# The last pair of blocks of the down product as rounded parts and rests, for experts 1 to 5, and list products in another order

## The chip, the cores and the metric

The kernel runs on one core of a Trainium2 chip. The metric is the device time of one execution in microseconds (us), as the median of three runs.

## What is computed

A cross-attention layer with heads mixed before and after the softmax, and then a layer of eight experts with a balanced assignment, on two batches of 1024 rows of 256. Cut to what matters:

```
# attention: 16 heads of 64, context of 64 rows
attn = einsum(q, k); attn = einsum(attn, Wth1); attn = softmax(attn); attn = einsum(attn, Wth2)
x = x + einsum(einsum(attn, v), Wo)

# experts: E = 8, T = 2048 rows, each expert takes the 256 best of those not yet taken
y = layernorm(x); norm = layer_norm(y, ln_g, ln_b); scores = norm @ centroids.T
for e in range(E):
    s = where(taken, -inf, scores[:, e]); idx = top_k(s, 256); taken[idx] = True
h = layer_norm(y[idx of e], ln_g, ln_b)
h = gelu(h @ w1[e] + b1[e]) @ w2[e] + b2[e]          # 256 -> 1024 -> 256
x[idx of e] = x + y + h
```

## The kernel before

The program has a block per engine; each engine runs its own list of instructions in order and waits for semaphores of the others. There is no planner: the order is written out by hand in loops.

**Preparation and attention.** Fills (`for f in range(LATE)` on PE, ScalarE and VectorE) make the products of the key and value weights with the context, the head mixing, and their splits. `centre(h)` takes the mean out of the query weights: VectorE sums four blocks (L787), scales the sums (L789) and adds them to two blocks (L792), ScalarE to the other two (L608). Copies out of PSUM are by turns ScalarE's (even f) and VectorE's (odd f). Behind its copy f = 5 VectorE makes `mix` and two casts. Then come 16 tiles of 128 rows, in a pipeline of steps. In the last tiles VectorE counts the leading bytes of expert 0's scores: `count_bytes(t)` adds a comparison of 256 thresholds to `hist` for one tile; `first_totals()` on PE sums `hist` over the partitions, and `first_two()` on VectorE finds the first two digits of the threshold from the sum.

**The expert stage.** A loop `for k in range(SLOTS)`, written out, runs on PE, VectorE, ScalarE and GpSimd (POOL); I call one pass a round. In round k, expert k's threshold is searched (8 steps r, each `compare` on VectorE, `total` on PE, `narrow` on VectorE; `select` and `ranks` at the end), expert u = k - 1 gets its list and its rows, and expert e = k - 2 gets its up and down products. Round 7 has no search; its list follows from what is left.

The list of an expert: VectorE's `lists` makes `Hoh` and `Loh` (L1114); POOL's `token_rows` makes `Htk` of them (L505); PE's `tokens` multiplies both (waits for Htk), VectorE's `lists_out` masks (L1121), PE's `spread` spreads, VectorE's `indices` makes `idx` (L1126, L1130); POOL's `gather` starts two gathering DMAs (L516). The rows are transposed on PE (L1491, two halves, in steps 4 and 5), scaled by ScalarE into `yT` and `yF` (L713), and POOL subtracts for the rests (`y_rest`, L532).

A product in f32 "by parts": an operand is split into a rounded part (type fp32r) and a rest, and `mm3` (all PE products have line L1233) multiplies rounded by rounded, rounded by rest and rest by rounded. The up products of all experts are by parts: ScalarE's `w1_high` rounds w1 (L700), POOL's `w1_rest` subtracts in four instructions of 128x512 (L526). The down products of experts 0 to 5 are whole f32 products of `hT` and `w2s`, 16 per expert (two halves `a` of the rows, eight blocks `f`), laid over steps 2 to 8 by `DOWN`. Those of experts 6 and 7 (`parted`) are by parts, from `hp` and `w2p`: ScalarE writes gelu into a PSUM bank, and VectorE's `hidden_split` makes both parts from there (L1148, L1150), as `w2_rest` does for w2 (L1138).

POOL's order in a round k with u between 1 and 6: `token_rows(u)`, `w1_rest` 0, `gather(u)`, `w1_rest` 1 to 3, `y_rest(u)`, `bias(u)` (L540), `scatter(k - 3)` (two DMA issues, L547). ScalarE's: `hidden` of the later blocks (Gelu, L742), `w1_high(k)`, `rows(u)`, `hidden` of the first blocks of u. Memory of the experts: `hT` has two buffers by parity, `w2s` too; w2 of expert e is loaded (L408) when expert e - 2's down products are done.

## Time and profile before

| | |
|---|---|
| median of 3 runs | 309.21 us (308.43 to 309.61) |
| profiled execution | 308.5 us, of which the span from the first to the last instruction is 306.7 |
| granted TensorE clock, mean | 0.992 of full speed |
| busy: PE, PE's weight loads | 287.6 us (94%), 249.2 us (81%) |
| busy: VectorE, ScalarE, POOL | 233.1 (76%), 148.7 (48%), 197.5 us (64%) |
| chain that ended last | PE 77%, VectorE 8%, POOL 5%, DMA 4% |

Preparation lasts to about 51 us, attention to 162, the expert stage to the end. Busy time is that in which an instruction of the engine is under way; matmuls overlap, so twelve with 280 ns each take far less than twelve times that, and the pace is the distance of their starts. "Idle before" and the name behind an arrow say how long the engine stood before an instruction and who let it go on.

### The profile page before, as it was taken

To read this page: it belongs to the slowest core of one execution; us is meant where nothing else is said; L and a number is where in the kernel's file an instruction comes from. 1 tells how busy PE (TensorE), PEld (TensorE's weight loads), DVE (VectorE), ACT (ScalarE), POOL (GpSimd) and SP (SyncE) were. 2 spreads that over 40 slices of the span, in tenths; PEclk is the share of its full clock that TensorE was granted. 3 is DMA by queue.
4 is the path that set the end of the run, shared out by engine and by line. 5 is a ranking of instruction groups with operands and counts; after the bars stand their busy time and mean duration, and the time that the engine had idled before them with its cause. 6 is when DMAs were issued, how large, how long until landed. Compare 5 with 4: busy or idle time off the path is not lost.

```text
span 306.7 us, 6418 instructions
## 1 busy us (share of the span) xinstructions
PE 287.6 (94%) x2034; PEld 249.2 (81%) x2034; DVE 233.1 (76%) x808; ACT 148.7 (48%) x267; POOL 197.5 (64%) x247
## 2 busy tenths in 40 slices
PE   6999999999999999999988779999999999999990
PEld 2989998999999999999983228797979797989990
DVE  0579879999988888888877878687878787548650
ACT  1257646355445555555546523535353545474720
POOL 8200213468987888876742785758788878787951
PEclk9999999999999999999999999999999999999996
DMA  6996000991001000000016330474737474622020
GB/s 254 357 366 229 1 2 17 366 335 39 35 34 37 34 34 34 34 34 34 34 71 205 115 94 1 97 250 104 275 102 276 118 260 134 246 68 71 34 79 26
DMA packets 21770, 37.85 MB, mean 123 GB/s; under 512 B 2417, under 2 KB 14961, under 8 KB 21361
## 3 DMA queue, kind: packets, MB, share of 16 engines
q1 hardware_dynamic: 19184, 31.22, 29.4%
q0 software_dynamic: 2560, 6.31, 6.8%
q8 instruction: 14, 0.23, 0.3%
q14 instruction: 12, 0.09, 0.1%
HBM read 31.23 MB, written 6.29 MB: 122 GB/s over the span
## 4 chain that ended last, share of the span: by engine, by line
PE 77%; DVE 8%; POOL 5%; DMA 4%; issue 3%; ACT 1%; SPq 0%; POOLq 0%; DVEq 0%
PE pair L1233 67%; PE pair L1309 4%; PE pair L1283 2%; DMA wk_s<-wk_dram 2%; DVE cmpb L1019 1%; POOL w2p L556 1%; PE pair L1491 1%; DMA G<-rows_scratch,idx 1%; PE pair L1321 1%; POOL G L516 1%; DMA out_dram<-G,idx 1%; DVE wneg L787 1%; POOL out_dram L547 1%; POOL yT L532 1%; PE pair L1449 1%
## 5 line engine op out<-in xcount | busy, mean ns | idle before, releaser
L1233 PE MATMUL pair<-yT,w1p 128*128 128x256 f32 x384 | 53.2, 289 | 0.2
L1233 PE MATMUL pair<-Bm,pT 128*128 128x256 f32 (+1 forms) x384 | 49.9, 285 | 0.2 <-ACT pT L634 0.2
L1233 PEld LDWEIGHTS pair<-yT,w1p 128*128 128x128 f32 x384 | 48.3, 189 | 1.0 <-POOL yT L532 0.3
L1233 PE MATMUL pair<-Am,xTp 128*128 128x512 f32 (+1 forms) x192 | 48.9, 402 | 0.0
L1233 PE MATMUL pair<-w2s,hT 128*128 128x256 f32 x192 | 47.2, 389 | 0.0
L1233 PEld LDWEIGHTS pair<-Bm,pT 128*128 128x128 f32 x384 | 46.6, 188 | 0.4 <-issue 0.4
L288 POOL TENSOR_TENSOR pr<-pr,rs 128x1024 f32<-128x1024 f32 (+1 forms) x16 | 31.2, 1951 | 21.9 <-DVE rs L877 15.3
L526 POOL TENSOR_TENSOR w1p<-w1s,w1p 128x512 fp32r<-128x512 f32 x32 | 40.0, 1276 | 5.7 <-ACT w1p L700 5.6
L1233 PEld LDWEIGHTS pair<-Am,xTp 128*128 128x128 f32 x192 | 35.0, 189 | 7.0
L742 ACT ACTIVATE hT<-pair,b1s 128x256 f32<-128x256 f32 x48 | 20.1, 470 | 34.6 <-PE pair L1233 34.6
L1233 PEld LDWEIGHTS pair<-w2s,hT 128*128 128x128 f32 x192 | 33.5, 191 | 4.2
L469 POOL TENSOR_TENSOR xTp<-xTs,xTp 128x256 fp32r<-128x256 f32 x16 | 11.9, 741 | 33.8 <-ACT xTp L601 33.8
L629 ACT ACTIVATE pr<-pr,r 128x1024 f32<-128x1024 f32 x16 | 18.4, 1152 | 27.9 <-DVE pr L922 27.9
L516 POOL DMA_INDIRECT G<-rows_scratch,idx x16 | 15.8, 984 | 15.2 <-DVE idx L1130 12.8
L1019 DVE TENSOR_SCALAR_CACHE_REDUCE cmpb<-pair 128x256 bf16<-128x256 f32 x48 | 23.5, 489 | 1.7
L918 DVE TENSOR_REDUCE mx<-pair 128x16 f32<-128x1024 f32 x16 | 19.5, 1218 | 4.2 <-PE pair L1233 4.0
L883 DVE TENSOR_TENSOR pT<-pair,pT 128x512 fp32r<-128x512 f32 x32 | 21.3, 669 | 0.3 <-ACT pT L634 0.3
L922 DVE TENSOR_TENSOR pr<-pair,mx 128x1024 f32<-128x1024 f32 x16 | 19.6, 1225 | 2.0 <-DVE mx L918 1.3
L870 DVE TENSOR_REDUCE sm<-pr 128x16 f32<-128x1024 f32 x16 | 19.3, 1206 | 1.3 <-ACT pr L629 1.1
L547 POOL DMA_INDIRECT out_dram<-G,idx x16 | 15.8, 989 | 6.8 <-issue 3.1
L713 ACT ACTIVATE yT<-pair,gbs 128x256 fp32r<-128x256 f32 x16 | 8.2, 559 | 23.8 <-PE pair L1491 23.8
L1233 PE MATMUL pair<-ones_b 128*128 128x512 bf16 x61 | 17.9, 413 | 1.5 <-DVE ones_b L776 1.5
(157 smaller groups left out, 571.3 us busy)
## 6 DMA issues: line engine op xcount, KB each, us to landing
w1s<-w_dram SPq DMA_DIRECT2D x8, 1024.0 KB, 5.0
w2s<-w_dram SPq DMA_DIRECT2D x7, 1024.0 KB, 6.2
rows_scratch<-row SPq DMA_DIRECT2D x16, 256.0 KB, 2.0
xs<-x_dram SPq DMA_DIRECT2D x1, 2048.0 KB, 16.7
xTs<-xT_dram SPq DMA_DIRECT2D x1, 2048.0 KB, 18.4
wk_s<-wk_dram SPq DMA_DIRECT2D x1, 1024.0 KB, 6.0
wv_s<-wv_dram SPq DMA_DIRECT2D x1, 1024.0 KB, 8.3
wqT_s<-wqT_dram SPq DMA_DIRECT2D x2, 512.0 KB, 9.7
```

What stands on the lines that cost most here:

```text
L288: return eng.tensor_tensor(p4, p4, rs[:, v, :].unsqueeze(1).unsqueeze(3).to_broadcast([P, end - first, H, K8]), ALU.mult)
L516: pool.indirect_dma_start(out=G[:, b, a, :], out_offset=None, in_=rows_dram, in_offset=bass.IndirectOffsetOnAxis(ap=idx[:, e, a:a + 1], ax ...
L526: nc.gpsimd.tensor_tensor(w1p[:, 1, v, c, half], w1s[:, v, c, half], w1p[:, 0, v, c, half].bitcast(f32), ALU.subtract).then_inc(e_w1l, 1)
L547: pool.indirect_dma_start(out=out, out_offset=bass.IndirectOffsetOnAxis(ap=idx[:, e, a:a + 1], axis=0), in_=G[:, b, a, C:], in_offset=None ...
L629: nc.scalar.activation(pr[:, v, :], pr[:, v, :], ACT.Exp, scale=r1[:, ds(t, 1)]).then_inc(s_exp, 1)
L742: nc.scalar.activation(to, bank[1 + g % 2][:, h * CAP:(h + 1) * CAP], ACT.Gelu_apprx_tanh, bias=b1s[:, e * FC + f:e * FC + f + 1]).then_in ...
L870: nc.vector.tensor_reduce(sm[:, v, :], pr[:, v, :].rearrange("p (g i k) -> p i g k", g=KG, i=H), AX.XY, ALU.add).then_inc(s_sum, 1)
L883: nc.vector.tensor_tensor(pT[:, 1, v, q], probs_bank(t, g)[:], pT[:, 0, v, q].bitcast(f32), ALU.subtract).then_inc(s_pTs, 1)
L918: nc.vector.tensor_reduce(mx[:, v, :], pair[v][:].rearrange("p (g i k) -> p i g k", i=H, k=K8), AX.XY, ALU.max).then_inc(s_mx, 1)
L922: nc.vector.tensor_tensor(pr[:, v, :].rearrange("p (g i k) -> p g i k", i=H, k=K8), pair[v][:].rearrange("p (g i k) -> p g i k", i=H, k=K8 ...
L1019: nc.vector.tensor_scalar(cmpb[:], search_bank(k)[:, 0:T2 * P], thr.bitcast(f32), 0.0, ALU.is_ge, ALU.add, accum_out=cntb[:]).then_inc(r_c ...
L1233: return nc.tensor.matmul(out_, l, r, start=start, stop=stop)
```

## The change

- **Down products.** For experts 1 to 5 (`quarter`), the blocks f = 6 and 7 of the down product are by parts, 2 x 2 products of three instructions each in place of whole f32 ones. `LAST_DOWN`, which puts block 0 of the second half ahead of blocks 6 and 7 of the first, holds for them too.
- **Their parts.** ScalarE applies bias and gelu to the two blocks twice: first into `hp` (rounded, places 4 to 7 by parity), then into `hT` as before. VectorE subtracts (`pair_rest`, in step 4 of round e + 2, behind `compare` and `turn`). ScalarE rounds the pair of w2 behind `w1_high` (with a wait for the load of w2), POOL subtracts (`w2_pair_rest`, behind `w1_rest` 3 and ahead of `y_rest`, in round e + 1). PE waits for both in `down`.
- **Waits for shared places.** `hidden_split` of expert 6's third and fourth pair and `w2_part(7, 2)` wait for the end of expert 5's down products.
- **Lists.** In round 2, `spread` follows the up product of block 6 and not of block 5. In round 7, `tokens` comes behind the last two down products and the first two up products of expert 6 (part 8) and not ahead of them, and `spread` behind part 9 and not ahead of it.
- **Preparation.** Of the first four blocks of query weights, ScalarE centres three and VectorE one (two and two before). `mix` and the two casts come behind copy f = 11.
- **First digits.** The last tile's comparison goes into `atleast` alone; PE sums `hist` of the other 15 tiles, and then `atleast` on top.

```diff
@@ gpsimd
+            def w2_pair_rest(e, v):
+                q = quarter_place(e)
+                pool.wait_ge(e_qh, e)
+                nc.gpsimd.tensor_tensor(w2p[:, 1, 1, q], w2s[:, v, FC - 2:FC], w2p[:, 1, 0, q].bitcast(f32),
+                                        ALU.subtract).then_inc(e_ql, 1)
...
+                        if quarter(e):
+                            w2_pair_rest(e, v)
@@ scalar
-                for j in (4 * h + 2, 4 * h + 3):
+                for j in (1, 2, 3) if h == 0 else (6, 7):
...
+                if quarter(e) and g == FC // 2 - 1:
+                    for h in range(2):
+                        f = 2 * g + h
+                        nc.scalar.activation(hp[:, 0, 4 + v * 2 + h, :], bank[1 + g % 2][:, h * CAP:(h + 1) * CAP],
+                                             ACT.Gelu_apprx_tanh,
+                                             bias=b1s[:, e * FC + f:e * FC + f + 1]).then_inc(e_hq, 1)
...
+                if quarter(u):
+                    act.wait_ge(e_w2[u % 2], 16 * (u // 2 + 1))
+                    nc.scalar.activation(w2p[:, 1, 0, quarter_place(u)], w2s[:, u % 2, FC - 2:FC], ACT.Copy).then_inc(e_qh, 1)
...
+                        act.wait_ge(e_o, ST * PARTED)
                         w2_part(u, 2)
@@ vector
-                for j in (4 * h, 4 * h + 1):
+                for j in (0,) if h == 0 else (4, 5):
...
-                if f == 5:
+                if f == 11:
...
-            count_bytes(x)
+            dve.wait_ge(s_sc, T)
+            dve.wait_ge(r_hist, T - 1)
+            nc.vector.tensor_scalar(atleast[:], dig[:, 0, :], S[:, 0, x:x + 1], 1.0, ALU.is_le, ALU.mult).then_inc(r_last, 1)
...
-                if e > PARTED:
+                if e > PARTED or g >= 2:
                     dve.wait_ge(e_o, ST * e)
...
+            def pair_rest(e):
+                q = quarter_place(e)
+                dve.wait_ge(e_hs, FC * (e + 1))
+                dve.wait_ge(e_hq, 2 * e)
+                nc.vector.tensor_tensor(hp[:, 1, q, :], hT[:, e % 2, FC - 2:FC, :], hp[:, 0, q, :].bitcast(f32),
+                                        ALU.subtract).then_inc(e_hl, 1)
...
+                    if r == 4 and quarter(k - 2):
+                        pair_rest(k - 2)
@@ tensor
-                            pe.wait_ge(s_wcA, m // 2 + 2)
-                            pe.wait_ge(s_wcD, m // 2 + 2)
+                            pe.wait_ge(s_wcA, 3 if m == 0 else 5)
+                            pe.wait_ge(s_wcD, 1 if m == 0 else 3)
...
-                pe.wait_ge(r_hist, T)
-                mm(bank[5][:, 0:FIRST], ones_b[:, 0:P], hist[:], True, True).then_inc(r_first, 1)
+                pe.wait_ge(r_hist, T - 1)
+                mm(bank[5][:, 0:FIRST], ones_b[:, 0:P], hist[:], True, False)
+                pe.wait_ge(r_last, 1)
+                mm(bank[5][:, 0:FIRST], ones_b[:, 0:P], atleast[:], False, True).then_inc(r_first, 1)
...
-                if e == E - 1:
+                if e == E - 1 or quarter(e):
                     n = LAST_DOWN[n]
...
-                if parted(e):
+                if quarter(e) and f >= FC - 2:
+                    q = 4 + v * 2 + f - (FC - 2)
+                    pe.wait_ge(e_ql, e)
+                    pe.wait_ge(e_hl, e)
+                    last = mm3(bank[4 + a][:, 0:C], lambda i: hp[:, i, q, a * P:(a + 1) * P], lambda i: w2p[:, 1, i, q, :],
+                               False, f == FC - 1)
+                elif parted(e):
...
-                        if e == 0:
-                            list_of_tokens(k, gap, 1 - f % 2)
+                        if e == 0 and f == 5:
+                            list_of_tokens(k, gap, 0)
                         up(e, f)
                         if e > 0:
                             list_of_tokens(k, gap, f % 2)
+                        elif f == 6:
+                            list_of_tokens(k, gap, 1)
...
-                if k == E - 1:
-                    tokens(k)
                 expert_part(k, 8)
...
                 if k == E - 1:
-                    spread(k)
+                    tokens(k)
                 if searches(k):
                     ranks(k)
                 expert_part(k, 9)
+                if k == E - 1:
+                    spread(k)
```

The renaming of the loop variable `quarter` to `n` in `w1_rest` changes nothing.

## Rows read from the trace of the kernel before

**Rows 1.** The chain that ended last: start, us, what; the last turn from POOL to PE
```profile
268.16 3.56 DMA G<-rows_scratch,idx
271.77 0.44 PE pair L1491 x2
```
**Rows 2.** Busy time by stretch: us, engines with instructions, clock, DMA share, GB/s; round 5
```profile
233.82:248.92 15.10, 15.06 (x100) 12.95 (x100) 11.60 (x71) 7.10 (x14) 12.34 (x13) 1.00 0.59 189
```
**Rows 3.** Timeline of POOL, round 5: start, us, instruction, count, idle before and releaser
```profile
233.82 0.64 POOL L505 TENSOR_TENSOR Htk<-Hoh,cst 128x256 fp32r<-128x256 f32 x1
...
236.72 1.00 POOL L516 DMA_INDIRECT G<-rows_scratch,idx  x1 [1.02 <-DVE idx L1130]
...
239.00 3.72 POOL L526 TENSOR_TENSOR w1p<-w1s,w1p 128x512 fp32r<-128x512 f32 x3
243.65 1.41 POOL L532 TENSOR_TENSOR yT<-yF,yT 128x256 fp32r<-128x256 f32 x2 [0.93 <-ACT yF L713]
```
**Rows 4.** Timeline of PE, round 5: the product tokens, and the down products of step 5
```profile
234.51 0.44 PE L1233 MATMUL pair<-Htk,Loh 128*128 128x128 f32 x2
...
240.71 1.03 PE L1233 MATMUL pair<-w2s,hT 128*128 128x256 f32 x4
```
**Rows 5.** Timeline of PE: whole f32 down products in a row, and down products by parts
```profile
272.04 2.32 PE L1233 MATMUL pair<-w2s,hT 128*128 128x256 f32 x10
...
292.94 6.10 PE L1233 MATMUL pair<-w2p,hp 128*128 128x256 f32 x48
```
**Rows 6.** One line's instructions (ns least/median/most, when); timeline of POOL beside such subtractions
```profile
L1166 DVE TENSOR_TENSOR yT<-yF,yT x2: 412/938/1465, 285.4 to 286.7; 128x256 fp32r<-128x256 f32 x2
...
285.24 1.29 POOL L526 TENSOR_TENSOR w1p<-w1s,w1p 128x512 fp32r<-128x512 f32 x1
...
184.36 0.92 POOL L540 TENSOR_TENSOR G<-G,b2s 128x256 f32<-128x256 f32 x1
```
**Rows 7.** Single lines' instructions: ScalarE's Gelu and its copy of 128x512
```profile
L742 ACT ACTIVATE hT<-pair,b1s x48: 464/472/476, 186.3 to 267.8; 128x256 f32<-128x256 f32 x48
...
L727 ACT ACTIVATE w2p<-w2s x4: 633/638/641, 274.1 to 286.7; 128x512 fp32r<-128x512 f32 x4
```
**Rows 8.** Round 5: VectorE's turn in step 4; ScalarE's rows; a DMA issue's us to landing
```profile
240.06 0.16 DVE L1029 TENSOR_TENSOR pair<-pair,ics 128x1 int32<-128x1 int32 x1
...
242.10 1.02 ACT L713 ACTIVATE yT<-pair,gbs 128x256 fp32r<-128x256 f32 x2 [2.09 <-PE pair L1491]
...
w2s<-w_dram SPq DMA_DIRECT2D x7, 1024.0 KB, 6.2
```
**Rows 9.** Timeline of rounds 7 and 8, several engines
```profile
269.14 3.73 POOL L526 TENSOR_TENSOR w1p<-w1s,w1p 128x512 fp32r<-128x512 f32 x3
...
270.62 1.03 PE L1233 MATMUL pair<-w2s,hT 128*128 128x256 f32 x4
...
270.70 0.41 DVE L1114 TENSOR_TENSOR Loh<-cst,pair 128x256 fp32r<-128x256 f32 x1
...
276.77 4.49 PE L1233 MATMUL pair<-yT,w1p 128*128 128x256 f32 x36
...
282.87 0.69 DVE L1150 TENSOR_TENSOR hp<-pair,hp 128x512 fp32r<-128x512 f32 x1
...
283.61 3.80 PE L1233 MATMUL pair<-w2p,hp 128*128 128x256 f32 x30
```
**Rows 10.** Timeline of the preparation: VectorE's centring, PE's query and output weights
```profile
13.31 0.61 DVE L792 TENSOR_SCALAR wqT_s<-wqT_s,wneg 128x256 f32<-128x256 f32 x2
...
16.25 2.95 PE L1233 MATMUL pair<-kvT,wqT_s 64*128 64x128 f32 x48 [0.37 <-ACT wqT_s L608]
...
19.51 3.84 PE L1233 MATMUL pair<-kvT,wo_s 64*128 64x128 f32 x64 [0.31 <-DVE AB L813]
```
**Rows 11.** Timeline of PE at the end of the attention: the six filling products
```profile
161.21 1.46 PE L1233 MATMUL pair<-ones_b 128*128 128x512 bf16 x6
```
**Rows 12.** Timeline of PE, round 2: the product spread(1)
```profile
189.82 0.33 PE L1233 MATMUL pair<-Rt,exp_r 128*128 128x128 f32 x1 [0.47 <-DVE Rt L1121]
```

More of the change, by code:

```diff
@@ L193, in build @@
         r_R, r_Rt, r_Rx, r_Rxm = sem("r_R"), sem("r_Rt"), sem("r_Rx"), sem("r_Rxm")
-        r_idx = sem("r_idx")
+        r_idx, r_last = sem("r_idx"), sem("r_last_bytes")
         r_hist, r_hist0, r_first, r_firstj, r_firsts, r_atl = (sem("r_" + n) for n in ("hist", "hist_cleared", "first_totals", "first_sum", "first_state", "at_least"))
@@ L199, in build @@
         e_g = [sem(f"gathered{i}") for i in range(GB * ST)]
+        e_qh, e_ql, e_hq, e_hl = sem("w2_pair_high"), sem("w2_pair_rest"), sem("hidden_pair_high"), sem("hidden_pair_rest")
         e_yD = sem("first_rows_rest_dve")
@@ L246, in parted, with quarter, quarter_place @@
             return e >= PARTED
+        def quarter(e):
+            return 1 <= e < PARTED
+        def quarter_place(e):
+            return slice(4 + e % 2 * 2, 6 + e % 2 * 2)
         def part(e, kind, n):
@@ L519, in gather, with w1_rest @@
                     ).then_inc(e_g[ST * b + a], 16)
-            def w1_rest(e, v, quarter):
-                if quarter == 0:
+            def w1_rest(e, v, n):
+                if n == 0:
                     pool.wait_ge(e_w1h, e + 1)
-                c, half = quarter // 2, slice(quarter % 2 * F // 2, (quarter % 2 + 1) * F // 2)
+                c, half = n // 2, slice(n % 2 * F // 2, (n % 2 + 1) * F // 2)
                 nc.gpsimd.tensor_tensor(w1p[:, 1, v, c, half], w1s[:, v, c, half], w1p[:, 0, v, c, half].bitcast(f32),
                                         ALU.subtract).then_inc(e_w1l, 1)
+            def w2_pair_rest(e, v):
[3 more added lines that the diff above has]
+                                        ALU.subtract).then_inc(e_ql, 1)
             def y_rest(e, v):
@@ L561, in _ @@
                 if k == 0:
-                    for quarter in range(W1_PARTS):
-                        w1_rest(0, 0, quarter)
+                    for n in range(W1_PARTS):
+                        w1_rest(0, 0, n)
                     early_w2_rest(0)
@@ L575, in _ @@
                         if e > 0:
-                            for quarter in range(1, W1_PARTS):
-                                w1_rest(e, v, quarter)
+                            for n in range(1, W1_PARTS):
+                                w1_rest(e, v, n)
+                        if quarter(e):
+                            w2_pair_rest(e, v)
                     if e == E - 2:
@@ L585, in _ @@
                     if e == E - 2:
-                        for quarter in range(W1_PARTS):
-                            w1_rest(E - 1, (E - 1) % 2, quarter)
+                        for n in range(W1_PARTS):
+                            w1_rest(E - 1, (E - 1) % 2, n)
                 if 0 <= k - 3 < E:
```

## The prediction, made before the changed kernel was run

> **What bounds the kernel now.** I read the chain that ended last first, then the busy time by stretch, then the timeline of each engine in one round of the expert stage. A round is the piece in which one expert is searched for, the one before it gets its token list and rows, and the one before that its products. TensorE (PE) is busy nearly all of a round, 15.06 of 15.10 us, against 11.6 for VectorE (DVE), 7.1 for ScalarE (ACT) and 12.3 for GpSimd (POOL) [rows 2]. Read as shares, that says that PE is the bound and POOL has 2.8 us to spare. The chain says otherwise: its last stretch runs through POOL (the rest of the rows, the scatter issue, Htk, the gather), then through the gather's landing, and only at 271.77 back to PE, which stays on it to the end [rows 1]. So I follow POOL's queue. From Htk at 233.82 to the next at 248.92 it has two waits of size: 1.02 us before the gather, and 0.93 us before the rests of the rows [rows 3]. Everything behind the second follows without idle time, and the next Htk is ready just when PE wants it: PE's list product stands at 234.51, 0.05 after the end of its round's Htk (233.82 + 0.64) [rows 3, 4]. What POOL loses beyond 0.93 us in a round, PE therefore waits for.
>
> The wait before the gather can't absorb anything: it lies behind Htk, on the path Htk, PE's list product, DVE, PE's spreading product, DVE's indices, gather, and this path, 2.90 us from Htk to gather (236.72 - 233.82), moves along with Htk. POOL's own ring is thus 15.10 - 0.93 = 14.17 us, not 12.3.
>
> **Gain: the products.** A whole f32 product takes two instructions. Ten in a row take 2.32 us, less the last one's 0.38, over nine steps: 0.216 each, 0.432 for a product. Three products of parts: 48 instructions in 6.10, less 0.28, over 47: 0.124 each, 0.372 [rows 5]. For 4 products in each of 5 experts: 20 x 0.060 = 1.20 us of PE time less. This is worth something only where PE is the last to arrive. The Trainium skill (FP8 and Floating Point Precision, TensorE Precision Notes) counts a true f32 product as four passes; three instead of four would make it 0.324 and save 2.2 us in all. The rows have 0.372, and I go by them.
>
> **Cost: POOL.** w2_pair_rest adds one subtraction of 128x512 per round, put behind the last three of w1_rest. Those three take 3.72 us, a step of 1.24 [rows 3]. The wait of 0.93 behind them takes the most of it; 0.31 us are over.
>
> **Cost: the port between DVE and POOL.** pair_rest is a DVE subtraction with both inputs in SBUF (hT and hp). hidden_split keeps one of its inputs in PSUM, and so do nearly all of DVE's in this stage. The trace has three of the new kind. L1166's first took 1465 ns and its second 412: the first, at 285.4, began while POOL was in w1_rest (285.24, 1.29 long), and ended about 0.3 after that one's end. The third, L1157, came between two instructions of POOL, and the second of them took 0.92, where two of its size take 1.41 together [rows 3, 6]: 0.2 more. So each waits for the other. For 128x512 DVE takes 0.69, 0.28 more than the 0.41 of 128x256 [rows 6, 9]: it ends 0.3 + 0.28, say 0.55, behind POOL's end, and POOL's next one is stretched by 0.2 + 0.28, say 0.47. pair_rest stands in the fourth part of the round, behind the comparison (DVE free at 240.2), in the midst of POOL's three subtractions (239.00 to 242.72) [rows 3, 8]. It is nearly a tie with the end of the first (240.28). I take it that DVE gets in there: done at 240.83, against PE's wish for it at 240.71 [rows 4]; the search chain slips by 0.2 to 0.3, which hides behind POOL.
>
> **Sum per round.** 0.31 + 0.47 = 0.8 us more than before, and PE's savings of 0.24 then only lengthen its wait. Rounds 3 to 6 have both additions. In round 3 (behind the Htk at 202.67) the order of things is the same, but PE had some 0.1 us to spare, so 0.65. Sum 0.65 + 3 x 0.8 = +3.05. Without the port's part it would be 0.2 + 3 x 0.31 = +1.15.
>
> **Round 7** (the last expert's list; no search). DVE's Loh ends at 271.12, pair_rest follows, and POOL's three subtractions (269.14 to 272.87) are under way; its second ends at 271.64, so pair_rest at 272.19. PE wants expert 5's pair at 270.62 and now comes to it at 272.25, needs two products (0.75), and is at the second half of the rows at 273.0, where it was at 271.77 [rows 1, 9]: +1.2 (without the port: 271.8, +0.8). The last pair, two products, gives back 0.12.
>
> **The last expert's list moved.** tokens(7) goes behind two down and two up products, spread(7) behind two more up products. Behind the second half of the rows spread was at +4.9, just ahead of the up products of 276.77; it is now at 0.27 (the rows) + 5 x 0.43 + 2 x 0.37 + 4 x 0.72 + 0.3 (tokens) = +6.3, where 0.72 is an up product, six steps of 0.12 (36 instructions in 4.49, less 0.28, over 35). What hangs on it: DVE's indices, behind them four pairs of hidden_split, 1.44 us each, whose last ended at 283.56, 0.05 before PE took its part (283.61) [rows 9]. There is no slack, so PE is later by about 1.2 us; the gather comes later by as much and is hidden in this. Bounds 0.5 (if only the gather's lateness counted) to 1.4.
>
> **Preparation.** DVE centres one block instead of two before its second sum (two take 0.61): 0.27 sooner. ACT's third block fits in before PE's 14.7. PE's second half of the query weights starts 15.97 instead of 16.25. It works on them for 2.95, less the last instruction's 0.27, and so would be through at 18.95; but it waited until 19.51 for a DVE copy that stood behind mix and two casts, which now come later, where DVE otherwise waits for PE. PE goes on at 18.95 - 0.28 = 18.67: -0.84, bounds 0.6 (the casts alone) and 0.9 [rows 10]. Nothing in the attention stage but PE itself sets its pace, so the gain lasts.
>
> **Last bytes.** The sum over the histogram was due at 162.50 behind PE's six filling products (161.21, 0.213 each, end 162.49) [rows 11]. That it no longer waits for the last addition gains nothing, the second product costs 0.11. Bounds -0.1 and +0.2.
>
> **Round 2.** PE stood 0.47 us before spread(1) [rows 12]; now an up product (0.71) lies there. PE gains 0.6, but the gathered rows, 3.5 us behind their issue, arrive when they did: -0.45, bounds 0.3 and 0.6. w2_pair_rest(1) costs nothing: in this round POOL has no scatter yet, two issues less than in round 5, and waits for DVE's list.
>
> **ACT.** Two more Gelu (0.47 each) and one copy of 128x512 (0.64) per round: 1.58, in the 2.09 us in which ACT waited before the rows [rows 7, 8]. Nothing is queued behind it that is late; if that cover were gone, the rows and POOL's rests would slip. The copy's new wait is for w2's load, 6.2 us long [rows 8]. It is issued when the expert two before is done, a whole part before the round begins, and ACT comes to it behind w1_high, some 9 us later: nothing. The other new waits (hp and w2p of experts 6 and 7) are for expert 5's end, long past: nothing.
>
> **Total.** -0.84 + 0.11 - 0.45 + 3.05 + 1.2 - 0.12 + 1.2 = +4.15. On the profiled run (span 306.7, time 308.5) that is 312.65; on the median 309.21, 0.7 above it, 313.36. I forecast 313.0. The likeliest case with its own bounds: 311.9 to 314.0.
>
> **Rivals.**
> 1. *The tie goes to POOL.* If pair_rest is just too late for the gap at 240.28, it waits for POOL's second subtraction (241.50) and ends at 242.05. PE's pair, the next count and the second half of the rows come 1.44 us later, and POOL waits for the rows again: 1.44 a round instead of 0.8, 4 x 1.44 - 0.15 = 5.6 instead of 3.05: +6.7, 315.5. For it: DVE's turn ends at 240.22 and two waits stand before pair_rest. Against it: POOL's next instruction also needs its dispatch. The Trainium skill (SBUF: State Buffer, "SBUF: two separate sides") has it that whoever starts first holds the shared ports for its whole instruction; by that rule it is this case or the main one, and nothing between; L1166's 1465 agrees.
> 2. *The port costs nothing here* (pair_rest falls into POOL's waits or runs beside it). Only POOL's 0.31 per round: -0.84 + 0.11 - 0.45 + 1.15 + 0.8 + 1.2 - 0.12 = +1.85, 310.7. For it: three instructions are few. Against it: they all show it.
> 3. *Faster: POOL isn't the ring.* If POOL keeps up, by a wait that shrinks when the work behind it comes, PE gets its 1.20 us and the moved list costs nothing, because PE then has other work: -0.84 + 0.11 - 0.45 - 1.2 = -2.4, 306.4. It decides when a round's POOL work above today's stays under 0.93 us. For it: POOL's 12.3 of 15.1. Against it: the queue read out above.
> 4. *Little change*: POOL and DVE lose in some rounds only, and the gains pay for it: about 309.
>
> **How the numbers follow.** Main case 0.45 (313.0), first rival 0.14, second 0.17, third 0.17, fourth 0.07. The range from 309.0 to 316.0 leaves out the third and the far ends. What a measurement can tell from no change is 0.5%, 1.55 us: slower is above 310.8, faster below 307.7. The second rival lies on that edge, half of it to each side: faster 0.17, same 0.16, slower 0.67.
>
> **What would show it.** After: rounds of 15.9 us between the Htk of rounds 4 to 7, with no POOL wait before the rows' rests and a PE wait for Htk of 0.8; one POOL subtraction in each round at 1.7 us instead of 1.28; pair_rest at 0.7 to 0.8 (the tie lost: 1.9); the wo products at 18.7; spread(7) 6.3 us behind the rows. A POOL wait that is still there before the rests, or rounds under 15.1, would make the forecast wrong; so would hidden_split in time in spite of the later list.

## The result and the profile after

The changed kernel takes **331.1 us** (median of four runs, 331.0 to 331.9) against 309.07 us for the kernel before on the same chip (308.43 to 309.61): a ratio of 1.0719, 95% interval 1.0702 to 1.0736. The forecast was 313.0, in a range of 309.0 to 316.0. The direction was right; the size was five times too small.

The page of the kernel after (times in us, share of the span, count of instructions; TensorE's granted clock in tenths over 40 slices; the chain that ended last by engine; the group of the new product, with the idle time before it and who ended it):

```profile
span 330.1 us, 6511 instructions
...
PE 295.1 (89%) x2053; PEld 256.1 (78%) x2055; DVE 251.4 (76%) x812; ACT 155.7 (47%) x283; POOL 203.9 (62%) x252
...
PEclk9999999999999999999999999789799897999998
...
PE 76%; DVE 13%; POOL 3%; issue 3%; DMA 2%; ACT 0%; SPq 0%; DVEq 0%; POOLq 0%; ACTq 0%
```

Read it in the order of the page. PE is busy for 89% of a span that is 23.4 us longer. The clock, level over the first 25 slices, dips where the long rounds are. And the chain, which turned from POOL to PE in the kernel before [rows 1], now holds 13% of DVE. The chain's own pieces of one round say which DVE instruction that is:

```profile
249.07 0.18 DVE pair L1085
...
249.31 0.38 issue
...
249.85 4.26 DVE hp L1206
254.25 0.97 PE pair L1275 x7
255.21 0.37 PE pair L1535 x2
```

L1206 is pair_rest, the new subtraction, 4.26 us in the chain. All its instructions (ns: least, median, most; from when to when), and the view of the waits (us in total, times, the longest):

```profile
L1206 DVE TENSOR_TENSOR hp<-hT,hp x5: 2380/4330/4339, 207.9 to 291.2; 128x512 fp32r<-128x512 f32 x5
```
```profile
PE pair L1275 <- DVE hp L1206: 16.6, 5, 3.7
```

The same form with one input in PSUM takes 0.69 [rows 9]; this one takes 4.33 in rounds 3 to 6 and 2.38 in round 7, and PE waits for it 16.6 us in five times. The timelines of DVE, POOL and PE around the first of them (start, us, instruction, count, idle before and who ended it):

```profile
207.40 0.49 DVE L1051 TENSOR_SCALAR_CACHE_REDUCE cmpb<-pair 128x256 bf16<-128x256 f32 x1
...
207.89 4.32 DVE L1206 TENSOR_TENSOR hp<-hT,hp 128x512 fp32r<-128x512 f32 x1
212.13 0.16 DVE L1068 SCALAR_TENSOR_TENSOR ok<-pair,cst 128x16 f32<-128x16 f32 x1
```
```profile
206.72 3.71 POOL L534 TENSOR_TENSOR w1p<-w1s,w1p 128x512 fp32r<-128x512 f32 x3
210.40 1.25 POOL L541 TENSOR_TENSOR w2p<-w2s,w2p 128x512 fp32r<-128x512 f32 x1
216.13 1.41 POOL L547 TENSOR_TENSOR yT<-yF,yT 128x256 fp32r<-128x256 f32 x2 [4.47 <-ACT yF L730]
```
```profile
208.21 0.42 PE L1535 MATMUL pair<-cst,G 128*128 128x128 f32 x2
212.35 1.62 PE L1275 MATMUL pair<-w2p,hp 128*128 128x256 f32 x6 [3.73 <-DVE hp L1206]
```

pair_rest is issued at 207.89. POOL's row of four subtractions, w1_rest three times and w2_pair_rest, runs without a pause from 206.72 to 211.65, and pair_rest ends at 212.21, 0.56 behind its end. It is not let in between two of the four. POOL itself isn't slowed: three in 3.71, as in [rows 3]. PE stands from 208.6 to 212.35. Behind that POOL, which had 0.93 us to spare [rows 3], has 4.47: **it isn't the ring any more, DVE's one subtraction is.**

The busy time by stretch (length; PE, PEld, DVE, ACT, POOL with their instructions; granted clock, DMA share, GB/s): the stall of that round, the stretch behind it, and the whole next round, which answers to [rows 2]:

```profile
208.30:212.30 4.00, 0.32 (x4) 0.08 (x2) 4.00 (x3) 0.72 (x2) 3.35 (x3) 0.82 0.14 38
```
```profile
212.30:218.00 5.70, 5.65 (x19) 4.74 (x20) 2.59 (x16) 1.93 (x4) 1.87 (x3) 0.53 0.43 175
```
```profile
223.58:244.08 20.50, 16.80 (x106) 14.36 (x105) 15.74 (x72) 8.33 (x17) 13.53 (x15) 0.92 0.43 139
```

PE does almost nothing for 4 us, and then, busy without a break, works at a granted clock of 0.53, which is near the lower of its two levels, 1.2 GHz. After the stalls of rounds 4 to 6 the same stretch has 0.70 to 0.71. After the stall of round 7 (2.78 us) it stays at 1.00; that the length alone does not decide this is shown in the last section.

**Where the 23.4 us of the two profiled spans are** (product tokens, rows and end as marks, from the two timelines):

| stretch | before | after | difference |
|---|---|---|---|
| start to tokens of round 3 | 204.05 | 202.20 | -1.85 |
| rounds 3 to 6, tokens to tokens | 60.62 | 82.72 | +22.10 |
| round 7, to the second half of the rows of round 8 | 18.77 | 21.76 | +2.99 |
| from there to the end | 23.26 | 23.42 | +0.16 |

The first line has 0.61 us of an earlier landing of the weights in that execution, which is not the change's. The second holds nearly all: rounds of 21.38, 20.50, 20.51 and 20.33 instead of 15.31, 15.15, 15.10 and 15.06.

### The profile page after: what moved, and what is told of

The parts are those of the page before. It is cut to its first block, busy times and chain, and to the rows that moved or that the text cites. A ratio compares the mean times of both kernels' runs of the same rounds, so it can differ in the third digit from the quotient of the medians.

```text
span 330.1 us, 6511 instructions
## 1 busy us (share of the span) xinstructions
PE 295.1 (89%) x2053; PEld 256.1 (78%) x2055; DVE 251.4 (76%) x812; ACT 155.7 (47%) x283; POOL 203.9 (62%) x252
## 4 chain that ended last, share of the span: by engine, by line
PE 76%; DVE 13%; POOL 3%; issue 3%; DMA 2%; ACT 0%; SPq 0%; DVEq 0%; POOLq 0%; ACTq 0%
PE pair L1275 68%; DVE hp L1206 6%; PE pair L1351 4%; PE pair L1325 2%; DMA wk_s<-wk_dram 2%; DVE cmpb L1051 1%; POOL w2p L571 1%; PE pair L1363 1%; PE pair L1535 1%; DVE pair L1085 1%; POOL G L524 1%; DVE ok L1068 1%; POOL out_dram L562 1%; PE pair L1491 1%; POOL pr L296 0%
## 5 line engine op out<-in xcount | busy, mean ns | idle before, releaser
L1275 PE MATMUL pair<-w2s,hT 128*128 128x256 f32 x152 | 43.6, 438 | 0.0
L1275 PE MATMUL pair<-w2p,hp 128*128 128x256 f32 x156 | 22.6, 293 | 16.6 <-DVE hp L1206 16.6
L1275 PEld LDWEIGHTS pair<-w2s,hT 128*128 128x128 f32 x152 | 31.1, 222 | 5.5 <-issue 1.1
L1275 PEld LDWEIGHTS pair<-w2p,hp 128*128 128x128 f32 x156 | 20.0, 193 | 18.3 <-issue 17.6
L1068 DVE SCALAR_TENSOR_TENSOR ok<-pair,cst 128x16 f32<-128x16 f32 x54 | 9.3, 172 | 18.5 <-PE pair L1275 18.4
L547 POOL TENSOR_TENSOR yT<-yF,yT 128x256 fp32r<-128x256 f32 x13 | 9.2, 727 | 18.7 <-ACT yF L730 18.7
```

The lines of the kernel that those rows point to most:

```text
L1068: nc.vector.scalar_tensor_tensor(ok[:], search_bank(k)[:, A_TOT:A_TOT + NT], float(CAP), step_w[:, r, :], ALU.is_ge, ALU.mult, accum_out=a ...
L1275: return nc.tensor.matmul(out_, l, r, start=start, stop=stop)
```

## The experiments

The theory after the result: a DVE instruction with both inputs in SBUF can't run while POOL goes from one SBUF-reading instruction to the next without a pause; it waits for the end of the whole row. PE then waits for DVE, and its clock falls besides. The rivals: the subtraction is long for a reason of its own (its two tiles, its operand type, the number of its elements); or the time goes elsewhere (POOL's extra work, ACT's two extra Gelu, the last expert's list), and the long DVE instruction only fills a wait.

### A pause in POOL's row

After, with one wait more on POOL: its third subtraction of w1 doesn't start before pair_rest is done.

```diff
                             for n in range(1, W1_PARTS):
+                                if n == 2 and quarter(e - 1):
+                                    pool.wait_ge(e_hl, e - 1)
                                 w1_rest(e, v, n)
```

> The changed kernel with one wait more on POOL: before the third of its four w1_rest instructions it waits until pair_rest of the round is done. Theory P (the port): in the changed kernel pair_rest stands 4.3 us because DVE, with two inputs in SBUF, doesn't get in as long as POOL goes from one instruction to the next without a pause; with the pause it gets in behind the second w1_rest. pair_rest 0.7 to 1.3 us, rounds 15.7 to 16.3 us instead of 20.5, PE's clock not halved, time 312 to 315. Rival W (pair_rest waits for ScalarE's Gelu, or for something else that the new order brings): pair_rest stays at 4.3, and POOL loses as much: 331 or more.

Measured: 312.3 us (312.0 to 312.6), ratio to before 1.010 (1.0083 to 1.0117). All instructions of pair_rest, and one round's part of DVE's and POOL's timelines:

```profile
L1208 DVE TENSOR_TENSOR hp<-hT,hp x5: 680/714/730, 207.8 to 272.9; 128x512 fp32r<-128x512 f32 x5
```
```profile
223.82 0.72 DVE L1208 TENSOR_TENSOR hp<-hT,hp 128x512 fp32r<-128x512 f32 x1
```
```profile
222.70 1.29 POOL L534 TENSOR_TENSOR w1p<-w1s,w1p 128x512 fp32r<-128x512 f32 x1
...
224.62 2.52 POOL L534 TENSOR_TENSOR w1p<-w1s,w1p 128x512 fp32r<-128x512 f32 x2 [0.64 <-DVE hp L1208]
```

The same instruction on the same data, with all other work of the change in place, takes 0.71 instead of 4.33, and 18.8 of the 22.0 us are gone although a wait was added. So neither the tiles nor the type nor the other new work costs the time. This is also the forecast's main case made real: rounds of 16.14, 16.09, 16.08 and 16.10 against the 15.9 of the sum, and in the view of PE's waits the 0.8 each that the forecast names for Htk:

```profile
PE pair L1277 <- POOL Htk L513: 3.1, 4, 0.9
```

### One input in PSUM

After, with the second Gelu of the pair written to a bank of PSUM, from where pair_rest reads it; PE's next rows, which use that bank, wait for pair_rest.

```diff
+                    if quarter(e) and g == FC // 2 - 1:
+                        to = bank[0][:, h * CAP:(h + 1) * CAP]
...
-                nc.vector.tensor_tensor(hp[:, 1, q, :], hT[:, e % 2, FC - 2:FC, :], hp[:, 0, q, :].bitcast(f32),
+                nc.vector.tensor_tensor(hp[:, 1, q, :], bank[0].rearrange("p (f t) -> p f t", f=2),
...
+                if a == 0 and quarter(e - 1):
+                    pe.wait_ge(e_hl, e - 1)
```

> The changed kernel, but ScalarE's second Gelu of the pair goes into PSUM bank 0 (free at that time) instead of hT, pair_rest reads it from there, and PE's transposes into that bank wait for pair_rest. All waits on ScalarE and on the semaphores stay, DVE's subtraction has the same size, but only one input in SBUF. Theory P: pair_rest 0.69 us, PE waits 0.4 to 0.6 us a round, POOL's ring is 15.4: time 309.5 to 311.5. Rival W: pair_rest still over 3 us: 328 to 331. Rival Q (POOL's added work delays everything, the port doesn't matter): rounds stay near 20.

Measured: 311.1 us (310.2 to 312.8), ratio 1.0066 (1.0045 to 1.0088). DVE's and POOL's timelines in round 4:

```profile
223.98 0.68 DVE L1208 TENSOR_TENSOR hp<-pair,hp 128x512 fp32r<-128x512 f32 x1
```
```profile
222.87 3.75 POOL L534 TENSOR_TENSOR w1p<-w1s,w1p 128x512 fp32r<-128x512 f32 x3
```

Here POOL's row has no pause, and pair_rest lies in the midst of it and takes 0.68. What held it was its second input in SBUF. Rounds are 15.45, 15.41, 15.93 and 15.86. In the last two the list comes later: PE waits 0.26 and 0.21 for DVE's Rt before `spread`, and POOL waits 1.53 and 1.47 before the gather, where it waits 1.01 in the round before them. I come back to this at the end.

### pair_rest and its product left out

After without the DVE subtraction and without the product that uses it (a part of the result is missing): what is left is POOL's and ACT's new work.

```diff
-                    if r == 4 and quarter(k - 2):
-                        pair_rest(k - 2)
...
-                    pe.wait_ge(e_hl, e)
-                    last = mm3(...)
+                    pe.wait_ge(e_hq, 2 * e)
+                    mm(bank[4 + a][:, 0:C], hp[:, 0, q, a * P:(a + 1) * P], w2p[:, 1, 0, q, :], False, False)
+                    last = mm(bank[4 + a][:, 0:C], hp[:, 0, q, a * P:(a + 1) * P], w2p[:, 1, 1, q, :], False, f == FC - 1)
```

> The changed kernel without pair_rest and without the product that uses it (the rest of the hidden pair by the rounded w2 is left out of the result); PE waits for the Gelu of the pair instead. Theory P: all of the loss goes, what stays is POOL's 0.3 us a round and the moved list: 308.5 to 311. Rival W: PE itself waits for the Gelu, 325 or more. Rival Q: unchanged, near 331.

Measured: 308.4 us (307.7 to 309.0), ratio 0.9974 (0.9963 to 0.9985), just under the 308.5 to 311 expected. Rounds: 15.44, 15.39, 15.39, 15.39. POOL's timeline in round 4, and PE's product tokens of the next:

```profile
222.13 3.73 POOL L534 TENSOR_TENSOR w1p<-w1s,w1p 128x512 fp32r<-128x512 f32 x3
225.83 1.27 POOL L541 TENSOR_TENSOR w2p<-w2s,w2p 128x512 fp32r<-128x512 f32 x1
227.07 1.41 POOL L547 TENSOR_TENSOR yT<-yF,yT 128x256 fp32r<-128x256 f32 x2
```
```profile
233.04 0.44 PE L1273 MATMUL pair<-Htk,Loh 128*128 128x128 f32 x2 [0.24 <-POOL Htk L513]
```

The wait of 0.93 before the rests of the rows [rows 3] is gone, and PE waits 0.24 for Htk. This is the forecast's reading of POOL as a ring: 14.17 + 1.24 = 15.41 was to come, and 15.39 to 15.44 came. The 2.8 us that POOL's busy share seems to leave free were not there.

### A small instruction in the same place

Before, with one DVE instruction more in that place of rounds 3 to 7: a subtraction of 128x16, both inputs in SBUF, whose result nobody uses.

```diff
+                    if r == 4 and 1 <= k - 2 < PARTED:
+                        nc.vector.tensor_tensor(probe[:], tok, iota, ALU.subtract)
```

> The kernel before with nothing but one DVE subtraction of 128x16 with two inputs in SBUF added in step 4 of rounds 3 to 7, where pair_rest stands (its result isn't used). Theory P: it is held from 240.2 until POOL's three w1_rest are through (242.7 in the trace of before), 2.5 us although it needs 0.1 by itself; the search chain and with it PE lose 2 us in each of four rounds, in round 7 little: 316 to 322 with what the clock adds. Theory P1 (the forecast's: it waits only for the instruction under way): 0.1 to 1.3 us: 309 to 311. Rival Q or W: 309.

Measured: 317.4 us (316.2 to 319.3), ratio 1.0287 (1.0259 to 1.0314). The instructions, and DVE's and POOL's timelines in round 4:

```profile
L1205 DVE TENSOR_TENSOR probe<-cst x5: 1861/2629/2647, 209.3 to 278.9; 128x16 f32<-128x16 f32 x5
```
```profile
226.35 2.63 DVE L1205 TENSOR_TENSOR probe<-cst 128x16 f32<-128x16 f32 x1
```
```profile
225.23 3.71 POOL L527 TENSOR_TENSOR w1p<-w1s,w1p 128x512 fp32r<-128x512 f32 x3
```

Sixteen columns, for which DVE's comparison just behind it (128x16, one input in PSUM) takes 0.16, take 2.63 us and end 0.04 behind POOL's row of three (225.23 + 3.71 = 228.94; 226.35 + 2.63 = 228.98). It was there 0.12 before the first of the three ended, and was passed over at two boundaries. The length is not that of the instruction but that of POOL's row. It costs 8.3 us although nobody waits for its result: DVE's search stands behind it, and the rounds are 17.17, 17.12, 17.12 and 17.56.

### A shorter row

After, with w2_pair_rest moved behind the rests of the rows: POOL's row has three instructions instead of four.

```diff
-                        if quarter(e):
-                            w2_pair_rest(e, v)
...
                     if e < E - 1:
                         y_rest(e, v)
+                    if quarter(e):
+                        w2_pair_rest(e, v)
```

> The changed kernel with w2_pair_rest behind y_rest on POOL instead of ahead of it, so that the unbroken row of POOL instructions over pair_rest is three long and not four. Theory P: pair_rest 4.33 - 1.25 = 3.1 us in rounds 3 to 6 (round 7 unchanged, 2.4), each of these rounds 1.2 to 1.5 shorter: 324.5 to 326.5. Theory P1 or W: pair_rest unchanged at 4.3.

Measured: 328.0 us (326.6 to 329.2), ratio 1.0602 (1.0571 to 1.0634). All instructions of pair_rest, and the first beside POOL's row:

```profile
L1206 DVE TENSOR_TENSOR hp<-hT,hp x5: 2386/3151/3157, 208.7 to 286.2; 128x512 fp32r<-128x512 f32 x5
```
```profile
208.74 3.11 DVE L1206 TENSOR_TENSOR hp<-hT,hp 128x512 fp32r<-128x512 f32 x1
```
```profile
207.57 3.72 POOL L534 TENSOR_TENSOR w1p<-w1s,w1p 128x512 fp32r<-128x512 f32 x3
```

One instruction of 1.24 less in the row makes pair_rest shorter by 1.18, and it again ends 0.56 behind the row (211.85 and 211.29). PE's waits for it fall from 16.6 to 11.7 us. The time was above the 324.5 to 326.5 expected: rounds of 19.29, 19.07, 19.41 and 18.97. The trace shows three parts of it. w2_pair_rest now lies behind POOL's wait for the rows and delays the next Htk: PE waits 1.18 and 1.33 us for it at the ends of rounds 4 and 6. In round 6 PE also waits 1.15 for the gathered rows. And the clock still falls (0.978 over the span, 0.969 in after), now in round 7 too.

### PE kept busy during its stall

After, with 17 filling products before PE's wait for pair_rest. Nothing uses them.

```diff
+                    if f == FC - 2 and a == 0:
+                        pe.wait_ge(e_hs, FC * (e + 1))
+                        keep_busy(17)
```

> The changed kernel with 17 filling products of ones (0.213 us each, 3.6 together) on PE just ahead of its wait for pair_rest in experts 1 to 5, so that PE isn't idle while DVE is held (the Gelu of the pair is waited for first). pair_rest stays at 4.3. What it tells apart is the stall and the clock: in the changed kernel the granted clock is 0.53 in the 5.7 us behind the first stall and 0.70 behind the next three, at most 2.7 + 3 x 1.7 = 7.8 us of PE time. If the clock is behind a part of the loss: clock 1.0 throughout, rounds 19.0 to 19.6 instead of 20.5, time 324 to 328. If the port's hold is all (the slower products are hidden behind the search chain): 330 to 331.

Measured: 325.5 us (325.3 to 325.8), and 307.9 for before on that chip (307.7 to 310.2): ratio 1.0556 (1.0511 to 1.0601), where after has 1.0719. Busy time of the stretch that holds stall and recovery:

```profile
206.00:222.00 16.00, 15.93 (x101) 12.13 (x101) 13.55 (x58) 6.55 (x12) 12.01 (x13) 1.00 0.57 179
```

pair_rest is as long as before (4.38 in the median), but the clock stays at 1.00, and rounds take 18.90 instead of 20.33 to 21.38. So the clock behind the stalls costs 1.6% or 5 us, by the two ratios (6.4 by the two spans). That is net of what the filling costs itself: rounds 3 to 6 are 7.1 us shorter together, round 7 is 0.8 longer. Without it a round is 3.8 longer than 15.1, which is the length of the stall.

### The change without its main part

After with quarter() always false: no products by parts in experts 1 to 5, only the moved lists and the preparation.

```diff
         def quarter(e):
-            return 1 <= e < PARTED
+            return False
```

> The changed kernel with no expert taken as quarter: whole f32 products for experts 1 to 5 as before; preparation, first digits, both lists moved stay. By the trace of the changed kernel up to round 3 these gain 1.3 to 1.9 us, and the list of the last expert costs 0.4 to 0.6 there: time 307.5 to 308.8. By the forecast's own sum (-0.84 + 0.11 - 0.45 + 1.2) it would be 309.1.

Measured: 309.25 us (308.7 to 309.6), ratio 0.9999 (0.9989 to 1.0008); 307.5 to 308.8 was expected. These parts bring nothing in sum, so all of the 22 us come from the products by parts. The miss has two sides. Its last expert's list costs 0.8. And its rounds 4 to 6 take 15.61, 15.59 and 15.55, 0.45 to 0.5 more than in the trace of before, though they are the same code; to this I come back below.

### The last expert's list alone

Before, with only tokens(7) and spread(7) moved.

```diff
-                if k == E - 1:
-                    tokens(k)
                 expert_part(k, 8)
...
-                if k == E - 1:
-                    spread(k)
+                if k == E - 1:
+                    tokens(k)
                 if searches(k):
                     ranks(k)
                 expert_part(k, 9)
+                if k == E - 1:
+                    spread(k)
```

> The kernel before with only the last expert's two list products moved as in the change (tokens behind part 8, spread behind part 9). Forecast's step: +1.2 us (310.2). By the trace of the changed kernel the way from the second half of expert 6's rows to that of expert 7's is 0.5 longer: +0.5 (309.6). Without the pair, the changed kernel measured 309.25, which with gains of 1.3 to 1.9 ahead of it would be a loss of 1.4 to 2 here.

Measured: 310.0 us (309.7 to 310.3), ratio 1.0027 (1.0018 to 1.0037): +0.9 us. It lies between the two sizes expected, 0.5 and 1.2.

### One input in PSUM, and the last expert's list as before

The kernel with one input in PSUM, and in it the four lines of the last expert's list put back:

```diff
+                if k == E - 1:
+                    tokens(k)
                 expert_part(k, 8)
...
-                if k == E - 1:
-                    tokens(k)
+                if k == E - 1:
+                    spread(k)
                 if searches(k):
                     ranks(k)
                 expert_part(k, 9)
-                if k == E - 1:
-                    spread(k)
```

> The change without its flaw as far as it can be mended: the pair's second Gelu in PSUM bank 0 (pair_rest not held) and the last expert's list where it was before. The list alone measured +0.87, the version with PSUM alone 311.1: 310.0 to 310.5, still above before (309.1), because POOL's ring is 0.3 us a round longer and PE waits for pair_rest 0.4. If it comes out under 308.5, PE's cheaper products do reach the end.

Measured: 308.8 us (308.2 to 309.4) beside 307.9 for before on that chip, ratio 1.0019 (1.0001 to 1.0037). Against the kernel with the list moved (1.0066) that is 0.5%, 1.5 us, somewhat more than the list alone; 310.0 to 310.5 was expected, from the times of another chip. The first three rounds, 15.41, 15.40 and 15.39, are again those of POOL's ring. The fourth takes 16.48, because the gathered rows land late for PE:

```profile
255.94 0.41 PE L1539 MATMUL pair<-cst,G 128*128 128x128 f32 x2 [1.44 <-DMA G<-rows_scratch,idx]
```

So even with no wait for the port the products by parts gain nothing here: POOL's ring sets three of the four rounds, and what PE saves in them does not reach the time. That the best possible form of them would gain nothing is not shown: why the rows of the fourth round land late was not found, and in round 7 PE waits 1.25 before the rows for pair_rest, by the wait that this version adds.

### The parts that gain, alone

Before, with both edits of the preparation and with spread(1) behind one more up product.

```diff
-                for j in (4 * h + 2, 4 * h + 3):
+                for j in (1, 2, 3) if h == 0 else (6, 7):
...
-                for j in (4 * h, 4 * h + 1):
+                for j in (0,) if h == 0 else (4, 5):
...
-                if f == 5:
+                if f == 11:
...
-                            pe.wait_ge(s_wcA, m // 2 + 2)
-                            pe.wait_ge(s_wcD, m // 2 + 2)
+                            pe.wait_ge(s_wcA, 3 if m == 0 else 5)
+                            pe.wait_ge(s_wcD, 1 if m == 0 else 3)
...
-                        if e == 0:
+                        if e == 0 and f == 5:
-                            list_of_tokens(k, gap, 1 - f % 2)
+                            list_of_tokens(k, gap, 0)
                         up(e, f)
...
+                        elif f == 6:
+                            list_of_tokens(k, gap, 1)
```

> The kernel before with the preparation's two edits (one block centred by DVE instead of two, mix behind copy 11) and spread(1) behind one more up product in round 2; whole f32 products, the last expert's list and the first digits as before. Forecast's steps: -0.84 and -0.45, so 307.8. The trace of the changed kernel shows the same sizes (0.9 and 0.5). If it stays above 308.8, one of the gains is given back later.

Measured: **308.0 us** (307.7 to 308.3), ratio 0.9960 (0.9947 to 0.9974). Among the versions that compute the whole result it is the one whose interval lies below 1, by 0.4%. PE's timeline of the query and output weights, which answers to [rows 10]:

```profile
14.38 4.07 PE L1233 MATMUL pair<-kvT,wqT_s 64*128 64x128 f32 x64
18.28 1.95 PE L1233 MATMUL pair<-kvT,wo_s 64*128 64x128 f32 x32
```

The query weights run through in one piece, and the output weights start 3.90 behind them, where it was 4.79. In all -1.07 us came where the forecast's steps for these edits give -0.84 - 0.45 = -1.29.

## Why the prediction was wrong in size, point by point

**The step that failed is the choice in "the port between DVE and POOL":** "I take it that DVE gets in there: done at 240.83". In after pair_rest begins at 249.76 in that round and takes 4.34. The forecast assumed that a boundary between two of POOL's instructions is a turn for DVE. The runs show that in an unbroken row of these subtractions it is none: held for 4.33 by a row of four, for 3.15 by a row of three, 2.63 even with sixteen columns, and 0.71 when the row has a pause. The first rival had the same flaw: it made DVE wait for one instruction more, never for all of them, so no case of mine contained the result. The rule that I cited from the Trainium skill (SBUF: State Buffer, "SBUF: two separate sides"), that the one who starts first holds the port for its whole instruction, agrees as far as it goes: with both inputs in SBUF no pair_rest ends beside a w1_rest (it ends 0.56 behind the row). But the measured hold is longer than one instruction (1.24), it is the whole row of four (4.33). I used the rule to say that it was this case or that "and nothing between"; the two were taken for the whole list.

**The evidence was misread.** Three instructions carried the conclusion [rows 6]. L1166's first, at 285.4, met the last of POOL's instructions in its row, so "0.3 after that one's end" could not tell "after the instruction" from "after the row". L1157 did come in between two, but of different lines (L532 and L540), not inside a row of like subtractions. What [rows 6] bear out is the size of the remainder, some 0.3 + 0.28 behind POOL's end: 0.55 was forecast, 0.56 measured. The upper bound should have been the rest of the row: from 240.2 to the end of four (239.00 + 4 x 1.24 = 243.96) and 0.55 behind it, 4.3 us a round instead of 0.6. That is what was measured, 4.33.

**The clock wasn't in the sum.** A stall of 3.7 us was in no case of mine, so neither was its sequel: a granted clock of 0.53 to 0.71 in the 5.7 us behind it. In all it costs about 5 of the 22 us. With the forecast's own stalls (0.8 for Htk) it stays up: 0.994 with the pause in POOL's row.

**The rest of the sum was near.** With DVE let in, the kernel takes 312.3, where 313.0 was forecast. That the two are so close is in part luck: the pause costs 0.64 a round where the port was put at 0.47, and the last expert's list 0.87 where it was put at 1.2. By its terms:
- POOL's queue, +0.31 per round: confirmed (rounds 15.39 to 15.44 without pair_rest, 15.41 by the sum), against the trace of before with its 15.10.
- The port when DVE gets in, +0.47 per round: POOL then lost 0.64, but by the wait put in, not by a stretched subtraction. In rounds 3 to 6 its own size couldn't be seen, since DVE never gets in without the pause. It shows once, in round 7 of after: there DVE gets in ahead of Htk, and Htk takes 1.07 instead of 0.62, 0.45 more.
- Round 7, +1.2 for pair_rest: with the pause PE waits 1.1. In after it is 2.78, since there too DVE is held to the end of the row: "its second ends at 271.64, so pair_rest at 272.19" is the same error.

```profile
291.19 2.38 DVE L1206 TENSOR_TENSOR hp<-hT,hp 128x512 fp32r<-128x512 f32 x1
```
```profile
289.29 3.71 POOL L534 TENSOR_TENSOR w1p<-w1s,w1p 128x512 fp32r<-128x512 f32 x3
292.97 1.07 POOL L513 TENSOR_TENSOR Htk<-Hoh,cst 128x256 fp32r<-128x256 f32 x1
```

- Preparation, -0.84: 0.89 from the query weights' start to the output weights' start.
- Last bytes, +0.11: from the histogram's product to tokens(0) 12.15 before, 12.26 after.
- Round 2, -0.45: tokens(1) to tokens(2) 15.87 before, 15.35 after, -0.52.
- The last expert's list, +1.2: mis-sized; +0.87 alone, though the place is right (spread(7) stands 6.17 behind the second half of the rows, 300.65 and 294.48; 6.3 was forecast).

```profile
294.48 0.38 PE L1535 MATMUL pair<-cst,G 128*128 128x128 f32 x2
...
300.65 0.22 PE L1275 MATMUL pair<-Rt,exp_r 128*128 128x128 f32 x1
301.23 3.12 PE L1275 MATMUL pair<-yT,w1p 128*128 128x256 f32 x24 [0.35 <-ACT pair L766]
```

- PE's 1.20 us: gained nowhere as time, as forecast. The third rival (faster, because POOL isn't the ring) falls with the run without pair_rest, where POOL is the ring.

**What would have shown it** was named: one POOL subtraction at 1.7 us, a POOL wait of nothing. After has neither (three in 3.71; waits of 3.62 to 4.47), and both signs point to where the step failed.

## What to carry to other kernels

Before a DVE instruction with two SBUF inputs is added, look at what POOL runs around it: if POOL has a row of SBUF-reading instructions without a pause, price it at the rest of the whole row, and give it one input in PSUM or put a real wait into POOL's row. Then ask who stands behind it on DVE and on PE, and what a stall of that length does to PE's clock: here the clock behind four stalls cost about 5 us on top of them. And read an engine's slack from its queue and its waits, not from its busy share: POOL's 12.3 of 15.1 us had room for 0.93, not for 2.8.

## What the runs showed of the hardware that was not expected

**DVE is shut out for a whole row.** The median in after, in the row of three and in the small instruction (4.33, 3.15 and 2.63 us) shows it, and those of which the timelines are shown end at the end of POOL's row plus a remainder (0.56, 0.56 and 0.04). When DVE does get in is only partly settled. It does not between two of w1_rest, nor between w1_rest and w2_pair_rest. It does before Htk in round 7 of after (292.97, where Htk takes 1.07 instead of 0.62), and it did before L540 in round 2 of before [rows 6], though by the order of the code nothing was left to wait for at Htk. What these boundaries have that the others lack stays open.

**The clock fell with the stalls, and their length does not say by how much.** PE was idle for 3.73, 3.63 and 3.75 us in rounds 3 to 5 of after; in round 6 it stood 0.90 for the rows and, after them, 2.71 for pair_rest. The 5.7 us behind had a clock of 0.53 in round 3 and of 0.70 to 0.71 in the others. In round 3 the clock fell while PE still stood (0.50 in the last 0.85 us of the stall), in rounds 4 to 6 only behind it. After 2.78 us, in round 7, it had 1.00. But in the kernel with the shorter row PE stood 2.52, 2.56 and 2.56 us in rounds 3 to 5 and had 0.70, 1.00 and 0.70 behind, and after 2.79 us in round 7 it had 0.72. Its stretches behind the stalls of rounds 3 and 4:

```profile
212.00:217.70 5.70, 5.70 (x26) 4.64 (x27) 2.96 (x20) 1.93 (x4) 2.87 (x4) 0.70 0.54 185
231.37:237.07 5.70, 5.63 (x37) 4.76 (x38) 4.51 (x29) 1.93 (x4) 2.89 (x4) 1.00 0.58 190
```

What decides between the two stays open. With filling products in the stall the clock was 1.00 in the stretches of 16 us around the stalls of rounds 3, 4 and 7.

**The same code runs at two paces.** Rounds 4 to 6 take 15.15, 15.10 and 15.06 in the trace of before, but 15.41, 15.54 and 15.52 in the kernel that differs from it only in the last expert's list, 15.61, 15.59 and 15.55 in the change without its main part, and 15.50, 15.59 and 15.56 in the version with the gaining parts alone. In the slower ones DVE's step behind the first count of a round begins 0.49 to 0.74 us behind the start of PE's sum, where it is 0.23 in before. The same step of round 6, in before and in the kernel with the list moved:

```profile
248.92 0.18 DVE L1036 SCALAR_TENSOR_TENSOR ok<-pair,cst 128x16 f32<-128x16 f32 x1 [0.46 <-PE pair L1233]
```
```profile
249.40 0.17 DVE L1036 SCALAR_TENSOR_TENSOR ok<-pair,cst 128x16 f32<-128x16 f32 x1 [0.92 <-PE pair L1233]
```

The list then comes later too, and POOL waits 1.43 to 1.50 before the gather instead of 1.01 (1.53 and 1.47 in the last two rounds of the version with one input in PSUM). That this wait lengthens the round by as much, while the one before the rests of the rows stays at 0.93, agrees with the forecast's reading that nothing can be hidden in it. Why DVE's step comes later wasn't found. The slower rounds 3 to 6 take 61.8 to 61.9 us together, against 60.62 in the table above, so some 1.2 of its 22.1 could be this and not the change. This bounds what a single trace can say of such a round: a term of a few tenths, taken from one execution, is not sure to hold in the next.
